# A gated two-layer block on one core: new order of ScalarE, VectorE and GpSimd work, and router logits in 16 products

## The chip, the cores and the metric

One NeuronCore of a Trainium2 chip runs the whole kernel. The metric is the time of the program on the device in microseconds. Three timed runs of the kernel before gave 561.67, 564.43 and 565.45 us; the median is 564.43.

## The reference

1024 tokens (4 x 256) of width 256 go through two layers, each an attention-like part and a feed-forward part, each part fed by a layer norm and added back through a tanh gate. Cut to what matters:

```python
x = x + tanh(g_xattn[0]) * _L0_xattn_ref(_layernorm(x), ids, ctx, ctx, ctx)   # 4 gated experts of 256, chosen by token id
x = x + tanh(g_ffn[0])   * _L0_ffn_ref(_layernorm(x), w_gate, w_up, w_down)   # BitNet: int8 tokens, ternary weights
x = x + tanh(g_xattn[1]) * _L1_xattn_ref(_layernorm(x), ctx, Wq, Wk, Wv, Wo)  # 8 x 128 tokens, 16 heads of 128
x = x + tanh(g_ffn[1])   * _L1_ffn_ref(_layernorm(x), gate_w, gate_bias, fc1_w, fc2_w, w1, w2, shared_up_w, shared_down_w)

# _L0_ffn_ref
gate = act_quant(x) @ weight_quant(w_gate).T         # act_quant: 128 / max|x| per token, rounded, clipped
up   = act_quant(x) @ weight_quant(w_up).T
y    = act_quant(fwht(silu(gate) * up)) @ weight_quant(w_down).T    # fwht: Walsh-Hadamard over 1024

# _L1_ffn_ref, 32 experts in 4 groups
scores = sigmoid(x @ gate_w.T)                       # the logits
sb     = scores + gate_bias
# per group: sum of the best two; the best two groups stay; of them the best 8 experts
cw     = scores of the chosen / their sum * 2.5      # 0 elsewhere
x_lat  = x @ fc1_w.T
h      = relu(x_lat @ w1[e].T)**2 * cw[:, e]         # for each of the 32 experts
out    = sum_e(h @ w2[e].T) @ fc2_w.T + relu(x @ shared_up_w.T)**2 @ shared_down_w.T
```

## The kernel before, in words

The tokens are NT = 8 tiles of 128, in NG = 2 halves of GN = 4 tiles (GT = 512 tokens). Each engine has a program of its own, written out in one function per engine, and they meet only at semaphores; an engine does its instructions in the order of the code. Matrices that must be exact to float32 are split into a high part (rounded to fp32r, mostly on ScalarE) and a low part (the rest, on VectorE or GpSimd), and one product is three TensorE passes: high by high, high by low, low by high (`product`, lines 1618 to 1624).

**Stages.** First the chosen experts of layer 0, then the BitNet feed-forward part, then 32 rounds u (16 heads by two halves of the batch) of attention, then 64 units i of the expert stage (32 experts for each half). The router and shared experts of the first half are done as tasks inside the last rounds of attention (`TASK_IN_STEP`), those of the second half inside the first units of the expert stage (`TASK_IN_UNIT`).

**Key/value units.** Beside the early stages TensorE computes keys and values of the attention, in units of 512 columns, numbered k. `FILLS` says how many units come behind which step of TensorE ("s0" to "d6"), and `FILL_AT[key]` which they are. TensorE's unit k waits for `kv_taken` >= k - 1, that is, until ScalarE (`take_unit`, the copy at L851) has copied the unit two before it out of the two PSUM banks they share. SyncE stores each copy (`store`), and the parts come back later as `k_hl` and `v_hl`, whose low parts are GpSimd's `key_low` (L598) and `value_low` (L604). Step "u0" waits for `y0_taken`, the last use of pair 0 in the stage before.

**Weight blocks.** All later weights come in 33 blocks of 512 KB in the order of `BLOCKS`: keys, values, queries, outputs, then the shared ones (S, D) and eight of the experts (E). For each, SyncE loads `blk_raw` (`load_block`, issued at L438, which waits until the block before is wholly taken), ScalarE makes the high part (`block_high`, L843) and GpSimd the low part (`block_low`, L592). Where each is done is written by hand in the feed-forward part, and by the tables `STEP_OF_BLOCK`, `UNIT_OF_BLOCK` (high), `LOW_UNIT_OF_BLOCK` (low) and `LOAD_AT_ROW` (the load, counted in rows `cw_row` of the router's weights that SyncE also loads, one per expert unit) later on. Blocks 29 to 32 hold the last sixteen experts.

**Feed-forward part.** Per tile there are TensorE stages: G (gate), U (up), H (the last Hadamard product), F (turn of the 1024 values into `fT`), C (the rounded values `q_b` turned back), D (down product); `STAGES` gives each its lag, and the list `FFN` the order, with the units "W" in between. ScalarE does silu (L954), `fT_hi` (L974) and `q` (L982); VectorE `inner` (`inner_values`, L1294), the maximum of the Hadamard result (L1434), `fT_lo`, `q_b` (L1457) and the update of `xr` (L1451); GpSimd the butterflies `fly` and `inner` (L650 to L656). The tokens of the first half are rounded by VectorE (`quantise(0)`); those of the second by ScalarE (`second_tokens`, L930), after VectorE's `token_scales(1)`, and TensorE turns them (L1836).

**PSUM pairs.** G, U, H, F and C each take a pair of banks from the list `free` in turn (`pair_of`), and before TensorE writes it waits for the one who used it last. While units stand behind "f1" no unit needs pair 0, so it is put into the list at ("W", "f1") and taken out at ("W", "d4"), where TensorE waits for its last user (`wait_freed(last_user[0])`).

**Router.** Task N normalises the tiles, L makes the logits (24 products of 32 columns per half: 4 tiles by 2 chunks by 3 passes), which ScalarE reads out of PSUM with its exponential (`logits_exp`); VectorE makes the scores (`scores_of_experts`), adds of the best two (`best_of_groups`), GpSimd the group mask (`mask_groups`, from L710), VectorE the best experts (`best_experts`), GpSimd the choice (`choose`), VectorE their sum (`wden`, L1392), GpSimd the weights `cw` (L744) and a root of them by Newton steps (L752 ends it), and task C turns them (L1998). They are stored (`store_weights`) and read back row by row. Tasks X and U are the latent tokens and the shared expert.

## Time and profile before

| | us |
|---|---|
| three timed runs | 561.67, 564.43, 565.45 |
| median | 564.43 |
| profiled execution, whole | 564.64 |
| its span (first to last instruction) | 562.8 |

All times in the rows below are of the profiled execution, counted from the start of its span. PE is TensorE (PEld its weight loads), DVE VectorE, ACT ScalarE, POOL GpSimd, and SPq the queue on which SyncE issues transfers. A wait is put down to the instruction whose end released it. PEclk is the granted clock of TensorE as a share of full speed, averaged over the window.

### The profile page before, as it was taken

The page shows a single profiled execution, that of the slowest core. Times are in us where ns is not written, and L with a number is a line of the kernel's source. Part 1 is how long each engine was busy: PE and PEld are TensorE (multiplying, and loading weights), DVE is VectorE, ACT ScalarE, POOL GpSimd, SP SyncE. Part 2 cuts the span into 40 slices and gives each one's busy share as a digit, 9 for nine tenths or more (in the row PEclk, how much of TensorE's full clock was granted, in tenths as well). Part 3 has the DMA queues.
Part 4 walks back from the last instruction along what each step waited for, and adds up shares of the span by engine and source line. Part 5 has one row for each costly group of instructions (what it writes and reads, how often), then busy time and mean ns, then how long its engine had stood idle before and what let it go on. Part 6 is the DMA issues. An engine that isn't in the chain of part 4 may idle for free.

```text
span 562.8 us, 9680 instructions
## 1 busy us (share of the span) xinstructions
PE 537.2 (95%) x3250; PEld 460.8 (82%) x3250; DVE 385.1 (68%) x815; ACT 355.4 (63%) x741; POOL 323.9 (58%) x325
## 2 busy tenths in 40 slices
PE   8999997998989999999999999999999989899997
PEld 6778765776778988998999999999999868677886
DVE  4858993699856576655655576636765857878883
ACT  4652245675678777766756565736766655787882
POOL 2679255899358697755645324425787465762320
PEclk9999998999999999999999999989999989999999
DMA  8911144610158677877577666524454745346751
GB/s 268 378 54 54 59 151 120 198 39 1 43 177 235 206 208 237 277 227 225 198 238 233 197 205 202 188 78 150 153 185 137 252 118 152 114 144 191 224 175 39
DMA packets 66544, 94.73 MB, mean 168 GB/s; under 512 B 6336, under 2 KB 38976, under 8 KB 66496
## 3 DMA queue, kind: packets, MB, share of 16 engines
q1 hardware_dynamic: 66496, 94.12, 52.6%
q8 instruction: 27, 0.44, 0.3%
q14 instruction: 21, 0.17, 0.1%
HBM read 66.71 MB, written 27.39 MB: 167 GB/s over the span
## 4 chain that ended last, share of the span: by engine, by line
PE 66%; DVE 17%; ACT 5%; issue 5%; POOL 4%; DMA 2%; SPq 0%; DVEq 0%; ACTq 0%; POOLq 0%
PE ps L1622 20%; PE ps L1623 19%; PE ps L1624 19%; PE ps L1754 4%; DVE xr L1230 2%; PE ps L1861 2%; DVE st L1135 1%; DMA xr<-in_x 1%; PE ps L1845 1%; DVE h L1165 1%; DMA cw_row<-cw_scratch 1%; DVE inner L1294 1%; DVE am L1434 1%; DVE e_lo L1547 1%; DVE e_r L1537 1%
## 5 line engine op out<-in xcount | busy, mean ns | idle before, releaser
L674 POOL TENSOR_TENSOR probs<-probs,rsum 128x512 f32<-128x512 f32 x64 | 66.6, 1044 | 57.6 <-DVE rsum L1318 57.5
L1313 DVE TENSOR_REDUCE nmax<-ps 128x2 f32<-128x512 f32 x64 | 44.0, 687 | 33.5 <-PE ps L1624 33.1
L1011 ACT ACTIVATE probs<-ps,nmax 128x256 f32<-128x256 f32 x128 | 59.9, 481 | 1.7 <-DVE nmax L1313 1.6
L1097 ACT ACTIVATE e_hi<-e_r 128x512 fp32r<-128x512 f32 x64 | 40.3, 629 | 31.0 <-DVE e_r L1537 30.0
L592 POOL TENSOR_TENSOR kv_w_lo<-blk_raw,kv_w_hi 128x1024 fp32r<-128x1024 f32 x16 | 38.8, 2424 | 36.2 <-ACT kv_w_hi L843 27.6
L1537 DVE SCALAR_TENSOR_TENSOR e_r<-ps,cw_row 128x512 f32<-128x512 f32 x64 | 43.6, 684 | 14.2 <-PE ps L1624 12.0
L1304 DVE TENSOR_TENSOR pT_lo<-ps,pT_hi 128x512 fp32r<-128x512 f32 x64 | 43.8, 685 | 12.8 <-ACT pT_hi L1017 12.2
L797 POOL TENSOR_TENSOR e_lo<-e_sq,e_hi 128x512 fp32r<-128x512 f32 x19 | 24.6, 1296 | 44.2 <-ACT e_sq L1103 39.3
L1309 DVE TENSOR_TENSOR oT_lo<-ps,oT_hi 128x512 fp32r<-128x512 f32 x32 | 22.1, 692 | 39.8 <-ACT oT_hi L1021 39.8
L1017 ACT ACTIVATE pT_hi<-ps 128x512 fp32r<-128x512 f32 x64 | 38.3, 601 | 15.8 <-PE ps L1754 15.6
L598 POOL TENSOR_TENSOR k_hl<-k_hl 128x512 fp32r<-128x512 f32 x20 | 26.0, 1298 | 37.1 <-ACT k_hl L938 37.0
L1021 ACT ACTIVATE oT_hi<-ps 128x512 fp32r<-128x512 f32 x32 | 19.1, 598 | 40.5 <-PE ps L1624 40.5
L1754 PE MATMUL ps<-eye,probs 128*128 128x128 f32 x256 | 39.0, 275 | 1.6 <-DVE kv_out L1344 1.0
L1622 PE MATMUL ps<-pT_hi,v_hl 128*128 128x256 f32 x128 | 36.7, 287 | 1.4 <-DVE hT_lo L1350 0.9
L853 ACT ACTIVATE kv_hi<-ps 128x512 fp32r<-128x512 f32 x36 | 21.7, 603 | 25.2 <-PE ps L1624 25.2
L1622 PE MATMUL ps<-k_hl,qT_lo 128*128 128x256 f32 x128 | 37.3, 291 | 0.0
L1624 PE MATMUL ps<-k_hl,qT_hi 128*128 128x256 f32 x128 | 36.3, 284 | 0.0
L1623 PE MATMUL ps<-wo_lo,oT_hi 128*128 128x256 f32 x128 | 36.2, 283 | 0.0
L1622 PE MATMUL ps<-wo_hi,oT_lo 128*128 128x256 f32 x128 | 36.2, 283 | 0.0
L1624 PE MATMUL ps<-pT_hi,v_hl 128*128 128x256 f32 x128 | 36.2, 283 | 0.0
L1623 PE MATMUL ps<-k_hl,qT_hi 128*128 128x256 f32 x128 | 36.2, 283 | 0.0
L1624 PE MATMUL ps<-wo_hi,oT_hi 128*128 128x256 f32 x128 | 36.2, 283 | 0.0
(311 smaller groups left out, 1873.6 us busy)
## 6 DMA issues: line engine op xcount, KB each, us to landing
cw_row<-cw_scratch SPq DMA_DIRECT2D x64, 256.0 KB, 3.4
v_hl<-v_scratch SPq DMA_DIRECT2D x24, 512.0 KB, 3.6
blk_raw<-in_w_blocks SPq DMA_DIRECT2D x22, 512.0 KB, 4.5
k_scratch<-kv_out SPq DMA_DIRECT2D x32, 256.0 KB, 2.6
v_scratch<-kv_out SPq DMA_DIRECT2D x32, 256.0 KB, 3.2
v_scratch<-kv_hi SPq DMA_DIRECT2D x24, 256.0 KB, 2.5
k_hl<-k_scratch SPq DMA_DIRECT2D x12, 512.0 KB, 3.5
k_hl<-k_scratch SPq DMA_DIRECT2D x20, 256.0 KB, 4.6
```

What stands on the lines that cost most here:

```text
L592: nc.gpsimd.tensor_tensor(lo[:, :], blk_raw[j % 2][:, :], hi[:, :].bitcast(F32), ALU.subtract).then_inc(blk_done, 1)
L674: nc.gpsimd.tensor_tensor(probs[:, b, :, :], probs[:, b, :, :], rsum[:, b, :].unsqueeze(2).to_broadcast([P, 2, S]), ALU.mult).then_inc(pro ...
L1011: last = nc.scalar.activation(probs[:, b, t, :], ps[:, S_BANK[b], t * S:(t + 1) * S], ACT.Exp, bias=nmax[:, b, t:t + 1], accum_out=esum[:, ...
L1017: nc.scalar.activation(pT_hi[:, b, :, :].rearrange("p k q -> p (k q)"), ps[:, P_BANK[b], :], ACT.Copy).then_inc(p_hi_done, 1)
L1097: nc.scalar.activation(e_hi[i % 4][:, :], e_r[i % 2][:, :], ACT.Square).then_inc(e_hi_done, 1)
L1304: V.tensor_tensor(pT_lo[:, b, :, :].rearrange("p k q -> p (k q)"), ps[:, P_BANK[b], :], pT_hi[:, b, :, :].rearrange("p k q -> p (k q)").bi ...
L1313: V.tensor_reduce(nmax[:, b, :], ps[:, S_BANK[b], :].rearrange("p (t k) -> p t k", t=2), AX.X, ALU.max, negate=True).then_inc(max_done, 1)
L1537: V.scalar_tensor_tensor(e_r[i % 2][:, :], ps[:, UP_BANK[i % 4], :], 0.0, cw_row[i % 4][:, :], ALU.max, ALU.mult).then_inc(root_done, 1)
L1622: mm(dst, l_lo, r_hi, start=first, stop=False, **kw)
L1623: mm(dst, l_hi, r_lo, start=False, stop=False, **kw)
L1624: return mm(dst, l_hi, r_hi, start=False, stop=last, **kw)
L1754: last = nc.tensor.transpose(ps[:, P_BANK[b], k * S + t * P:k * S + (t + 1) * P], probs[:, b, t, k * P:(k + 1) * P], ident)
```

## The change

The edits, by the names above:

1. **First tiles of the feed-forward part.** ScalarE no longer rounds the second tokens inside the units of "u1", but behind block 4, the first `fT_hi` and the first unit of "f0". VectorE's `token_scales(1)` is cut in two: the maximum (`token_maxima(1)`) first, then the first tile's low part (`turned_low(0)`), then the scales. `FILLS` moves the two units of "u0" to "g1" (three there), and with them the wait for `y0_taken`. Pair 0 enters `free` at place 2 instead of 0, so other stages use it.
2. **Scale of the Hadamard result.** The factor for `q` is min(128 / maximum, `c_most`) instead of being worked out from the clipped scale; `c_most` is new, one small operation per half.
3. **Blocks 5 to 7 and the key parts.** `BLOCKS` moves the first Q block from place 5 to 7. GpSimd does block 5 after tile 2, block 6 after tile 5 and nothing after tiles 3 and 6; `key_low(0)`, `key_low(1)` and `value_low(0)` come behind the last tile. ScalarE's `block_high(8)` moves from behind the queries to tile step 9, and the first turn of probabilities (`probs_back(0, 0)`) drops the wait for `kv_split`.
4. **Logits.** `gw_hi` and `gw_lo` lie side by side in `gw_hl`, 64 columns, so that a high token chunk meets both in one product: 16 products per half. VectorE adds the two column groups (`logits_add`, two operations, with a wait on the new `logit_added`), and ScalarE's exponential works in SBUF.
5. **Expert stage.** Tasks N, L, X and U stand at units 7, 9, 11, 12, 14, 16, 18 and 20 (before 6, 8, 10, 11, 13, 15, 17, 19), with the steps of VectorE, ScalarE and GpSimd for them one unit later; C stays at 23, as do `weight_sum` and the roots at 17. Blocks 29 to 32 are made at units 8, 9, 11, 13 (before 6, 7, 10, 16), and loads 31 and 32 issued at rows 15 and 17 (before 13, 16). `store_weights(1)` is issued before row 31, and its completion awaited before row 32.

The diff, cut:

```diff
-        BLOCKS = [("K", 0), ("V", 0), ("K", 1), ("V", 1), ("K", 2), ("Q", 0), ("K", 3), ("V", 2), ("O", 0), ("Q", 1), ("V", 3),
+        BLOCKS = [("K", 0), ("V", 0), ("K", 1), ("V", 1), ("K", 2), ("K", 3), ("V", 2), ("Q", 0), ("O", 0), ("Q", 1), ("V", 3),
...
-        UNIT_OF_BLOCK = {0: 28, 6: 29, 7: 30, 10: 31, 16: 32}
-        LOAD_AT_ROW = {4: 29, 8: 30, 13: 31, 16: 32}
+        UNIT_OF_BLOCK = {0: 28, 8: 29, 9: 30, 11: 31, 13: 32}
+        LOAD_AT_ROW = {4: 29, 8: 30, 15: 31, 17: 32}
...
-        FILLS = {"s0": 4, "s1": 2, "a11": 1, "y2": 1, "y6": 4, "u0": 2, "g1": 1, "u1": 3, "f0": 3, "g2": 1, "f1": 2, "d4": 1, "d5": 1, "c6": 1, "d6": 1}
+        FILLS = {"s0": 4, "s1": 2, "a11": 1, "y2": 1, "y6": 4, "g1": 3, "u1": 3, "f0": 3, "g2": 1, "f1": 2, "d4": 1, "d5": 1, "c6": 1, "d6": 1}
...
             if u == ("W", "f1"):
-                free.insert(0, 0)
+                free.insert(2, 0)
...
                 if n == 0:
                     block_low(4)
-                elif n in (2, 3):
-                    block_low(3 + n)
+                elif n == 2:
+                    block_low(5)
                 elif n == 5:
-                    key_low(0)
-                elif n == 6:
-                    value_low(0)
+                    block_low(6)

             pool.wait_ge(h_ready, NG + 1)
             block_low(7)
+            pool.wait_ge(q2_clipped, NT)
+            key_low(0)
             key_low(1)
+            value_low(0)
             block_low(8)
...
                     take("g" + str(i))
-                    if i == 1:
-                        second_tokens()
-                    else:
-                        take("u" + str(i))
+                    take("u" + str(i))
...
+                if i == NT + 1:
+                    block_high(8)
...
                 if i == 1:
-                    take("f0")
+                    take_unit(FILL_AT["f0"][0])
+                    second_tokens()
+                    for k in FILL_AT["f0"][1:]:
+                        take_unit(k)
...
                 if i == 1:
+                    last = token_maxima(1)
+                    turned_low(0)
+                    own(last)
                     token_scales(1).then_inc(q1_scaled, 1)
...
+                    own(V.reciprocal(a[:, 2:3], a[:, 0:1]))
+                    V.tensor_scalar(a[:, 2:3], a[:, 2:3], 128.0, c_most[:, n:n + 1], ALU.mult, ALU.min).then_inc(s2_ready, 1)
                     own(V.tensor_scalar(a[:, 1:2], a[:, 0:1], c_up[:, n:n + 1], Q_EPS, ALU.mult, ALU.max))
-                    own(V.reciprocal(a[:, 0:1], a[:, 1:2]))
-                    V.tensor_scalar(a[:, 2:3], a[:, 0:1], 128.0, c_up[:, n:n + 1], ALU.mult, ALU.mult).then_inc(s2_ready, 1)
...
-                    pe.wait_ge(kv_split, FILL_AT["e0"][-1] + 1 - FRONT_UNITS)
+                    if b:
+                        pe.wait_ge(kv_split, FILL_AT["e0"][-1] + 1 - FRONT_UNITS)
...
+            def logits_add(g, bank):
+                dve.wait_ge(logit_filled, g + 1)
+                parts = ps[:, bank, 0:2 * GN * E].rearrange("p (n two e) -> p n two e", n=GN, two=2)
+                own(V.tensor_copy(sc[:, :, :], parts[:, :, 0, :]))
+                V.tensor_tensor(sc[:, :, :], parts[:, :, 1, :], sc[:, :, :], ALU.add).then_inc(logit_added, 1)
...
+                        mm(ps[:, bank, wide], hT_hi[:, 0, tokens], gw_hl[:, 0, :], start=True, stop=False)
                         for c in range(DC):
-                            last = product(ps[:, bank, j * E:(j + 1) * E], both(hT_hi, hT_lo, A, c, slice(t * P, (t + 1) * P)),
-                                           both(gw_hi, gw_lo, A, c, A), c == 0, c == DC - 1)
+                            mm(ps[:, bank, narrow], hT_lo[:, c, tokens], gw_hl[:, c, 0:E], start=False, stop=False)
+                        last = mm(ps[:, bank, wide], hT_hi[:, 1, tokens], gw_hl[:, 1, :], start=False, stop=True)
```

**ScalarE, first two tiles.** Its rows from the second silu (`inner`) on, before; `kv_out` is the copy of a key/value unit, `qtok` the second tokens' rounding, `kv_w_hi` block 4.

```order
L954 ACTIVATE inner<-ps,c_gate 128x1024
L851 ACTIVATE kv_out<-ps 128x512 x2
L930 ACTIVATE qtok<-h,am_r 128x256 x4
L851 ACTIVATE kv_out<-ps 128x512 x2
L843 ACTIVATE kv_w_hi<-blk_raw 128x1024
L974 ACTIVATE fT_hi<-ps 128x1024
L851 ACTIVATE kv_out<-ps 128x512 x3
```

And now, from the first two silus on:

```order
L953 ACTIVATE inner<-ps,c_gate 128x1024 x2
L853 ACTIVATE kv_out<-ps 128x512 x6
L845 ACTIVATE kv_w_hi<-blk_raw 128x1024
L972 ACTIVATE fT_hi<-ps 128x1024
L853 ACTIVATE kv_out<-ps 128x512
L931 ACTIVATE qtok<-h,am_r 128x256 x4
L853 ACTIVATE kv_out<-ps 128x512 x2
```

The rounding moved from between the copies of "u1" to behind `fT_hi` and one copy of "f0"; the copies that stood between the two silus follow the second.

**GpSimd, end of the feed-forward loop.** Its rows behind the butterflies (`fly`, `inner`) of the sixth tile, before; `k_hl` and `v_hl` are key and value parts, `kv_w_lo` and `wq_lo` low parts of blocks.

```order
L598 TENSOR_TENSOR k_hl<-k_hl 128x512
L650 TENSOR_TENSOR fly<-inner 128x512
L651 TENSOR_TENSOR fly<-inner 128x512
L655 TENSOR_TENSOR inner<-fly 128x2x256
L656 TENSOR_TENSOR inner<-fly 128x2x256
L604 TENSOR_TENSOR v_hl<-v_hl 128x512
L650 TENSOR_TENSOR fly<-inner 128x512
L651 TENSOR_TENSOR fly<-inner 128x512
L655 TENSOR_TENSOR inner<-fly 128x2x256
L656 TENSOR_TENSOR inner<-fly 128x2x256
L592 TENSOR_TENSOR kv_w_lo<-blk_raw,kv_w_hi 128x1024
L598 TENSOR_TENSOR k_hl<-k_hl 128x512
```

And now, from the same place on:

```order
L593 TENSOR_TENSOR kv_w_lo<-blk_raw,kv_w_hi 128x1024
L651 TENSOR_TENSOR fly<-inner 128x512
L652 TENSOR_TENSOR fly<-inner 128x512
L656 TENSOR_TENSOR inner<-fly 128x2x256
L657 TENSOR_TENSOR inner<-fly 128x2x256
L651 TENSOR_TENSOR fly<-inner 128x512
L652 TENSOR_TENSOR fly<-inner 128x512
L656 TENSOR_TENSOR inner<-fly 128x2x256
L657 TENSOR_TENSOR inner<-fly 128x2x256
L593 TENSOR_TENSOR wq_lo<-blk_raw,wq_hi 128x1024
L599 TENSOR_TENSOR k_hl<-k_hl 128x512 x2
L605 TENSOR_TENSOR v_hl<-v_hl 128x512
```

A block's low part took the place of the key part behind the sixth tile, nothing stands behind the seventh, and both key parts and the value part come behind the last tile.

**GpSimd, expert stage of the second half.** Its rows at units 4 to 12, before; `e_lo` is its share of the expert values, `ex_lo` are blocks 31 and 32, `sbias` the biased scores, `gscore` the first step of `mask_groups`.

```order
L797 TENSOR_TENSOR e_lo<-e_sq,e_hi 128x512 x2
L592 TENSOR_TENSOR kv_w_lo<-blk_raw,kv_w_hi 128x1024
L592 TENSOR_TENSOR wo_lo<-blk_raw,wo_hi 128x1024
L797 TENSOR_TENSOR e_lo<-e_sq,e_hi 128x512 x2
L592 TENSOR_TENSOR ex_lo<-blk_raw,ex_hi 128x1024
L704 TENSOR_TENSOR sbias<-sc,gbias 128x128
L710 TENSOR_TENSOR gscore<-gtop 128x16
```

And now:

```order
L799 TENSOR_TENSOR e_lo<-e_sq,e_hi 128x512 x3
L593 TENSOR_TENSOR kv_w_lo<-blk_raw,kv_w_hi 128x1024
L593 TENSOR_TENSOR wo_lo<-blk_raw,wo_hi 128x1024
L799 TENSOR_TENSOR e_lo<-e_sq,e_hi 128x512
L593 TENSOR_TENSOR ex_lo<-blk_raw,ex_hi 128x1024
L706 TENSOR_TENSOR sbias<-sc,gbias 128x128
L593 TENSOR_TENSOR ex_lo<-blk_raw,ex_hi 128x1024
L712 TENSOR_TENSOR gscore<-gtop 128x16
```

Block 32's low part, which stood behind the masks and the best experts, now stands in front of `mask_groups`.

## Rows read from the trace of the kernel before

**Rows 1.** The page: busy time of each engine, its share of the span, instructions

```profile
PE 537.2 (95%) x3250; PEld 460.8 (82%) x3250; DVE 385.1 (68%) x815; ACT 355.4 (63%) x741; POOL 323.9 (58%) x325
```

**Rows 2.** TensorE's waits, by releaser: us in total, times, longest

```profile
PE ps L1622 <- ACT kv_out L851: 3.1, 1, 3.1
PE ps L1974 <- DVE h L1337: 2.4, 1, 2.4
PE ps L1622 <- DVE xr L1451: 2.0, 1, 2.0
...
PE ps L1622 <- DVE s_sq L1363: 1.4, 1, 1.4
...
PE ps L1754 <- DVE kv_out L1344: 1.0, 1, 1.0
...
PE ps L1836 <- issue: 0.7, 1, 0.7
PE ps L1622 <- DVE xr L1230: 0.7, 1, 0.7
```

**Rows 3.** Windows: length, busy PE, PEld, DVE, ACT, POOL, PEclk, DMA share, GB/s

```profile
90.00:100.00 10.00, 10.00 (x44) 7.37 (x44) 2.42 (x4) 5.37 (x8) 7.37 (x5) 0.83 0.61 158
360.00:380.00 20.00, 19.79 (x140) 18.43 (x139) 10.19 (x19) 10.82 (x30) 6.72 (x6) 0.91 0.40 132
440.00:460.00 20.00, 17.55 (x87) 14.20 (x86) 14.48 (x31) 12.32 (x21) 11.70 (x20) 0.91 0.58 177
460.00:480.00 20.00, 20.00 (x108) 16.90 (x108) 13.71 (x36) 12.46 (x22) 12.58 (x19) 1.00 0.52 156
```

**Rows 4.** Timeline, 78 to 90 us: start, duration, instruction, [idle before, releaser]

```profile
78.01 1.20 DVE L1146 TENSOR_SCALAR ln_i<-ln_v 128x4 int32<-128x4 int32 x1
...
85.78 1.21 DVE L1269 TENSOR_REDUCE am<-h 128x4 f32<-128x1024 f32 x1
...
87.45 1.70 ACT L930 ACTIVATE qtok<-h,am_r 128x256 f32<-128x256 f32 x4 [3.72 <-DVE am_r L1271]
```

**Rows 5.** Feed-forward loop: timeline, and `q_b` in ns min/median/max

```profile
117.97 1.11 ACT L982 ACTIVATE q<-ps,am 128x1024 f32<-128x1024 f32 x1
119.14 1.04 PE L1845 MATMUL ps<-wq,qT 128*128 128x512 bf16 x4 [0.46 <-ACT q L982]
135.05 1.27 POOL L604 TENSOR_TENSOR v_hl<-v_hl 128x512 fp32r<-128x512 f32 x1
...
L1457 DVE TENSOR_SCALAR q_b<-q x8: 682/1302/1764, 103.8 to 153.3; 128x1024 bf16<-128x1024 f32 x8
```

**Rows 6.** Timeline at the start of attention

```profile
160.75 2.40 POOL L592 TENSOR_TENSOR wo_lo<-blk_raw,wo_hi 128x1024 fp32r<-128x1024 f32 x1 [6.79 <-ACT wo_hi L843]
161.64 1.28 ACT L1011 ACT_TABLE_LOAD   x1
...
167.12 0.63 ACT L938 ACTIVATE k_hl<-k_hl 128x512 fp32r<-128x512 f32 x1 [0.78 <-DMA k_hl<-k_scratch]
```

**Rows 7.** TensorE's timeline, last output product, first and last of 24 logits products

```profile
367.75 0.28 PE L1624 MATMUL ps<-wo_hi,oT_hi 128*128 128x256 f32 x1
367.87 0.18 PE L1622 MATMUL ps<-gw_hi,hT_lo 128*128 128x32 f32 x1
...
370.36 0.26 PE L1624 MATMUL ps<-gw_hi,hT_hi 128*128 128x32 f32 x1
```

**Rows 8.** Expert stage: timeline; then loads (L438) from 400 us on, landing

```profile
461.06 0.33 SPq L438 DMA_DIRECT2D blk_raw<-in_w_tail  x1
475.43 0.22 POOL L710 TENSOR_TENSOR gscore<-gtop 128x16 f32<-128x16 f32 x1 [2.37 <-DVE gtop L1375]
484.68 2.30 DVE L1392 SCALAR_TENSOR_TENSOR wden<-wden 128x4 f32<-128x4 f32 x1
496.27 0.30 PE L1998 MATMUL ps<-eye,cw 128*128 128x128 f32 x1 [0.74 <-POOL cw L752]
...
DMA to landing us min/median/max: 3.2/5.6/6.6
```

More of the change, by code:

```diff
@@ L136, in flamingo_two_layer_kernel @@
         c_up = sb("c_up", [P, NT], F32, region)
+        c_most = sb("c_most", [P, NT], F32, region)
         qtok = sb("qtok", [P, GN, D], F32, region)
@@ L507, in _ @@
             load_block(4)
-            store("u0")
             load_block(5)
@@ L931, in second_tokens @@
                 last.then_inc(q1_rounded, 1)
-                for k in FILL_AT["u1"][1:]:
-                    take_unit(k)
             def key_high(u):
@@ L1025, in norm_chunk_high, with logits_exp @@
                 nc.scalar.activation(hT_hi[:, c, g * GT:(g + 1) * GT], ps[:, bank, :], ACT.Copy).then_inc(hT_hi_done, 1)
[L1027 to L1030 removed]
+            def logits_exp(g):
+                act.wait_ge(logit_added, g + 1)
+                nc.scalar.activation(sc[:, :, :], sc[:, :, :], ACT.Exp, scale=-1.0).then_inc(logit_exp, 1)
             def latent_high(g, bank):
@@ L1264, in _, with token_maxima @@
                 V.tensor_tensor(z_lo[:, g, :, :], a_sel[:, g, :, :], z_hi[:, g, :, :].bitcast(F32), ALU.subtract).then_inc(z_done, 1)
+            def token_maxima(g):
+                s = slice(g * GN, (g + 1) * GN)
+                return V.tensor_reduce(am[:, s], h[:, s, :], AX.X, ALU.max, apply_absolute_value=True)
             def token_scales(g):
                 s = slice(g * GN, (g + 1) * GN)
-                own(V.tensor_reduce(am[:, s], h[:, s, :], AX.X, ALU.max, apply_absolute_value=True))
                 own(V.tensor_scalar(am_c[:, s], am[:, s], Q_EPS, 1.0 / 128.0, ALU.max, ALU.mult))
@@ L1278, in quantise @@
                 else:
+                    own(token_maxima(0))
                     own(token_scales(0))
@@ L1285, in quantise @@
                 V.tensor_scalar(q1[:, :, :], qtok[:, :, :], ROUND, 127.0, ALU.subtract, ALU.min).then_inc(q1_ready, 1)
-                V.tensor_scalar(c_up[:, s], am_c[:, s], wmean[:, 1:2], None, ALU.mult)
+                own(V.tensor_scalar(c_up[:, s], am_c[:, s], wmean[:, 1:2], None, ALU.mult))
+                V.tensor_scalar(c_most[:, s], c_up[:, s], 128.0, 1.0 / Q_EPS, ALU.mult, ALU.mult)
                 V.tensor_scalar(c_gate[:, s], am_c[:, s], wmean[:, 0:1], None, ALU.mult).then_inc(scales_ready, 1)
@@ L1295, in inner_values, with turned_low @@
                                 ALU.mult).then_inc(inner_done, 1)
+            def turned_low(n):
+                b = pair_of["F", n]
+                dve.wait_ge(fT_hi_done, n + 1)
+                V.tensor_tensor(fT_lo[:, :, :].rearrange("p c t -> p (c t)"), ps[:, b:b + 2, :].rearrange("p a n -> p (a n)"),
+                                fT_hi[:, :, :].rearrange("p c t -> p (c t)").bitcast(F32), ALU.subtract).then_inc(fT_done, 1)
             def query_low(u):
@@ L1688, in fill_units @@
                         pe.wait_ge(a_taken, (NB - 1) * NG)
-                    if key == "u0":
+                    if key == "g1":
                         pe.wait_ge(y0_taken, NT)
```

76 lines of the change are left out of this document (37 added, 39 removed).

## The prediction

> **What bounds the kernel now.** I read the page's busy table first: TensorE is busy for 537 of 562.8 us [rows 1], so time falls only where TensorE gets less work, waits less, or runs at full clock. Next come TensorE's waits [rows 2]: the longest are 3.1 us for a ScalarE copy of a key/value unit, 2.4 us for the normalised tiles of the second half in the expert stage, 2.0 us for an update of `xr` at the end of the feed-forward part, 1.4 us for a `s_sq` and 1.0 us for a `kv_out`. Then the windows with the granted clock [rows 3]: it falls from 2.4 to 1.2 GHz behind the 3.1 us wait, and once more between 360 and 380 us, where TensorE hardly waited but had run the small router products. The loss is (1 - PEclk) times the window: 0.17 x 10 = 1.7 us between 90 and 100, 0.09 x 20 = 1.8 us between 360 and 380, and 1.8 us again between 440 and 460, behind the 2.4 us wait.
>
> The sum is made against the profiled execution, 564.6 us (span 562.8 and 1.8 around it); the median of the runs, 564.4, lies 0.2 below it, so I take the difference from 564.6. About 1%, 5.6 us, is what a measurement of this kernel can tell from no change.
>
> **1. First tiles (70 to 107 us).** Before, ScalarE's rounding of the second half's tokens stood in front of two unit copies: VectorE's maximum at 85.78 us, 1.2 us long, then scaling, then rounding from 87.45 for 1.7 us [rows 4]; the copies came after it, and TensorE, which may be two units ahead only, stood 3.1 us. Now ScalarE does all six copies, the block and the tile's high part first. Walking the new order with the old durations: unit copies to 85.4 us, block 4 to 86.4, `fT_hi` to 87.4, the first `f0` unit to 88.0; VectorE's low part to 88.7 and scales to 89.2; rounding (1.7) to 90.9; second `f0` unit to 91.5. TensorE reaches the `g2` unit, which needs that copy, at 90.6. So 0.9 of the 3.1 stays: 2.2 us won, and the clock's 1.7 with it, since no wait near its 3 us is left there (behind the 2.0 us wait the clock stayed). Units 12 to 14 move behind the second gate product, so the 0.7 us wait for VectorE's `xr` is filled with it, and the turn of the second tokens (`L1836`, 0.7 of issue) is no longer in pair 0, whose copy it waited for: 0.7 each. Sum 2.2 + 1.7 + 0.7 + 0.7 = **5.3 us**. Bounds: 3.0, if the wait only moves and the clock falls still; 7.0, if nothing is left of any wait.
>
> The scale reordering (reciprocal first, `c_most`) publishes the factor one small operation of 0.2 us earlier. In the loop it buys nothing: `q` starts at 117.97 behind ScalarE's own `fT_hi`, and TensorE's second product waits for that `q` until 119.14 [rows 5]. It counts once, at the last tile: 0.2 us. The added `c_most` is one such small operation per half, beside other waits; bounds 0 and 0.4.
>
> **2. End of the feed-forward loop (125 to 156 us).** The 2.0 us wait goes: pair 0 now ends with the last "up" result, which VectorE frees as it multiplies tile 7, and not with the `xr` update of tile 4, which is later in its queue. What is late next is GpSimd: block 6's low part (2.4 us) stands behind the sixth tile instead of a value part (1.3, [rows 5]), so the seventh tile's turn comes 1.1 us later, and with it the q of tile 5. Following it through: the last Hadamard product starts 0.7 us earlier than before. With the 0.2 above, **0.9 us**; bounds -1 and 2.5. The first key's two parts and the value's one (1.3 us each) and the Q block (2.4) come behind the tiles, where GpSimd was idle for 6.8 us [rows 6]; it walks to about 155 us for the first key, before the first scores. VectorE's `q_b` took 0.68 to 1.76 us for one shape [rows 5]; the last, 1.23 us, ran beside a key part that is now behind it. The Trainium skill, "SBUF — State Buffer", section "Who interferes with whom", says that a VectorE operation in a two-port mode and a GpSimd operation exclude each other for a whole instruction; the spread above agrees. It takes the last `q_b` to 0.7 us, which is hidden by ScalarE's `c6` copy and `hT_hi`, so the sum is the same by it.
>
> **3. Start of attention (159 to 168 us).** Block 8's high part (1.05 us) leaves the queue in front of the exponent table's load at 161.64 [rows 6] for an idle stretch of ScalarE near 150, and the first probabilities' turn drops its wait of 1.0 us for `kv_out`. Walked with the old durations, the probabilities are ready at 165.5 then, and TensorE comes to them at 166.4. But ScalarE next waits for a key load (0.78 us idle before 167.12), which comes no earlier; the slack behind it is about 1 us. **1.0 us**; bounds 0 and 2.
>
> **4. Logits.** 24 products of 32 columns start 0.108 us apart, (370.36 - 367.87) / 23 [rows 7], and one of 256 columns in front of them takes 0.12, so 64 columns cost nearly the same. Eight go: 0.87 us in each half. The Trainium skill, "TensorE: Matmul & The Clock Gate", section "Back-to-back issue gap", gives N / 2.4 GHz + 2.5 ns, an estimate of 16 ns for 32 columns; by it the eight would be worth 0.1 us. Its figure is not what the row shows here, and the row decides. The clock's fall behind them costs 1.8 us in the first half; the same 24 in the second half, between 460 and 480, ran at 1.00 throughout [rows 3]. I count it half gone: 0.9. First half **1.7 us**; bounds 0 and 2.7. The logits' sum on VectorE (two small operations) lies beside 1.4 us of expert products.
>
> **5. Expert stage of the second half (450 to 506 us).** On TensorE much goes: of the 2.4 us wait for the normalised tiles 0.9 stays, as one more expert unit (six products of 512 columns, by the 0.12 us of 256 columns in [rows 7] about 1.4 us) runs in front of the turn; the half clock behind it (1.8); 0.9 of logits; 1.4 for `s_sq`. But the router's result, the transposed weights at 496.27, sets the end, and GpSimd's `cw` released it after a wait of 0.74 [rows 8]. That chain runs logits, `sc`, masks (475.43 on), best experts, `wden` (484.68), roots. Walking it: block 29's low part ends near 464.5, not 461.0, so block 31's load is issued there. It lands in 3.2 us at best, as at 461.06, and 5.6 is the median of the seven from 400 us on. ScalarE, which reaches block 31 at 467.2, waits there, with logits' exponential and the latent high part queued behind it and VectorE waiting for them; scores at 471 to 472.4, the groups' best at 475.5, as before (475.4). Then GpSimd has block 32's low part (2.4 us) in front of the masks: they start at 478.3, 2.9 us late. What is given back: `wden` took 2.30 us beside a block's low part and now 0.3. Masks to 482.4, best to 483.6, choice to 485.4, `wden` to 486.9, exactly where it ended before. Roots are unchanged, 9 us. So the transposed weights stay at about 496.3: TensorE's gains turn into a wait there. What is left is the store of the weights before row 31 and its wait after it: **0.4 us**. Bounds: -3.5 (load of 6.6 us) and 5.5 (the chain not late at all).
>
> Sum: 5.3 + 0.9 + 1.0 + 1.7 + 0.4 = 9.3 us; 564.6 - 9.3 = **555.3 us**.
>
> **Rivals.**
> A (forecast): as above, 555.3, own range 552.5 to 558. Chance 0.50.
> B: the router's chain is not the bound, since blocks 31 and 32 get in between its steps; the expert stage then gives 1.5 (wait), 1.8 (clock), 0.9 (logits), 1.4 (`s_sq`), less the 0.4 counted: 5.2 more, 550.1. For it: `wden`'s 2.3 us collision goes. Against it: block 32 stands in GpSimd's queue before the masks. Chance 0.20.
> C: the first tiles give only their half. If GpSimd's block 4 holds up the two scaling operations on VectorE (such a small one took 1.20 us at 78.01 beside GpSimd [rows 4]), the rounding is 1.1 later, TensorE waits 2 us and the clock falls again (1.7); the late seventh tile eats the 0.9. 555.3 + 1.1 + 1.7 + 0.9 = 559.0. Chance 0.25.
> D, slower than before: one mechanism, ScalarE stopped at blocks 31 and 32 by their loads. It decides if both land in 6.6 us, the longest seen, instead of 3.2: 3.4 twice on the router's chain, and two falls of the clock at 1.7 behind TensorE's waits: 10.2 us, which is more than the 9.3 won; 565.5. Against it: few rows are in flight there. Chance 0.05.
> That the change does not do what it says: the 64-column products could cost more than the 32-column ones; between 0.108 and the 0.12 of 256 columns that is at most 0.1 us, so it has no case of its own.
>
> **Numbers.** Range 549.5 to 560.5: B's value at one end, C's with its spread at the other; D and the outer half of B are left out. Faster by over 1% (under 559.0): nearly all of A, all of B, half of C, 0.79. Within 1%: the rest of A and C, most of D, 0.18. Slower by over 1%: D with more on top, 0.03.
>
> **What would show it.** Step 1: no wait over 1 us and PEclk 1.00 between 85 and 100, the turn of the second tokens (`L1836`, second time) 5 to 6 us earlier than before. Step 2: no wait for `xr` L1451's successor, but `F` of tile 6 waiting for GpSimd. Step 3: the first turn of probabilities straight behind the scores. Step 4: 16 products in 1.8 us. Step 5: ScalarE idle before `ex_hi`, GpSimd's masks behind `ex_lo`, and a wait of 1 to 3 us before the transpose of `cw`. The forecast is wrong if the first wait is still over 2 us with a half clock behind it, or if the transpose of `cw` runs without a wait and over 4 us earlier relative to the start of the stage.

## The result, and the profile after

The changed kernel takes 555.05 us (median of four runs, 554.75 to 556.06) where before took 564.51 in the same session (four runs, 561.67 to 565.45): the medians lie 9.5 us apart. The ratio of the runs is 0.9842 (95% interval 0.9818 to 0.9865), which is 8.9 us. Its profiled execution took 554.95 us with a span of 553.2, 9.6 less than the span before.

TensorE's busy time fell by 4.4 us from [rows 1], to the line below. The other 5.2 of the 9.6 us were idle time:

```profile
PE 532.8 (96%) x3234; PEld 456.5 (83%) x3234; DVE 385.1 (70%) x821; ACT 354.3 (64%) x741; POOL 323.8 (59%) x325
```

TensorE's waits of the changed kernel (us in total, times, longest):

```profile
PE ps L1645 <- DVE xl_lo L1368: 2.0, 1, 2.0
PE ps L2024 <- POOL cw L754: 1.7, 1, 1.7
```

Of [rows 2] the 3.1 us for a unit copy, the 2.0 for `xr`, the 1.0 for `kv_out` and both 0.7 are gone, and the 2.4 for the normalised tiles has shrunk to 0.4; the 1.4 for `s_sq` is as before. New are 2.0 us for `xl_lo`, the low part of the latent tokens, and the wait for `cw` has grown from 0.7 [rows 8] to 1.7; both are in the expert stage. Windows that answer to [rows 3], with the same columns (PEclk is the third number from the end):

```profile
90.00:100.00 10.00, 9.98 (x60) 7.42 (x59) 8.32 (x12) 6.40 (x11) 8.49 (x8) 1.00 0.68 189
...
360.00:380.00 20.00, 20.00 (x141) 18.56 (x140) 12.11 (x24) 11.76 (x32) 8.24 (x8) 1.00 0.41 134
...
460.00:480.00 20.00, 16.55 (x65) 12.72 (x64) 16.44 (x51) 10.77 (x21) 13.26 (x26) 0.91 0.31 107
```

The clock stays at 2.4 GHz in the first tiles and behind the first half's logits (PEclk 1.00), and PEclk is 1.00 between 440 and 460 us too. In the expert stage it still falls once to 1.2 GHz for a time, only later, behind the 2.0 us wait (PEclk 0.50 between 464 and 466).

How much each stretch gave is read by taking the same instruction in both traces and subtracting its start. A "turn" is a transposition by TensorE:

| instruction on TensorE | before | after | gained so far | this stretch | forecast |
|---|---|---|---|---|---|
| first turn of second tokens | 105.06 | 99.66 | 5.40 | 5.4 | 5.3 |
| first product of the queries, behind the last `hT` | 156.02 | 149.46 | 6.56 | 1.2 | 0.9 |
| first turn of probabilities | 167.38 | 159.68 | 7.70 | 1.1 | 1.0 |
| first logits product | 367.87 | 360.22 | 7.65 | 0.0 | |
| last turn of probabilities | 431.92 | 421.83 | 10.09 | 2.4 | 1.7 |
| turn of `cw`, second half | 496.27 | 486.40 | 9.87 | -0.2 | |
| end of the span | 562.8 | 553.2 | 9.6 | -0.2 | 0.4 |

Two executions of unchanged code agree closely by this measure. Over the kernels below that share the changed kernel's first 99 us, that first turn lies between 99.46 and 99.67 in all but two (100.28 and 100.01, where everything from the first tiles on is shifted). From there to the first turn of probabilities they all take 60.0 or 60.1 us, and on to the first logits product 200.3 to 200.5 (experiments 8 and 12, whose edits lie in the first of these stretches, left out). So a difference in these stretches is good to 0.1 or 0.2 us, better than the whole times. It is not so later on. From the last turn of probabilities to the turn of `cw`, kernels with the same code there take 64.3 to 65.1 us, and from the turn of `cw` to the end 66.8 to 68.7 (the changed kernel and experiments 1 to 3, 8 and 12).

### The profile page after: what moved, and what is told of

The parts are those of the page before. It is cut to its first block, busy times and chain, and to the rows that moved or that the text cites. A ratio compares the mean times of both kernels' runs of the same rounds, so it can differ in the third digit from the quotient of the medians.

```text
span 553.2 us, 9654 instructions
## 1 busy us (share of the span) xinstructions
PE 532.8 (96%) x3234; PEld 456.5 (83%) x3234; DVE 385.1 (70%) x821; ACT 354.3 (64%) x741; POOL 323.8 (59%) x325
## 4 chain that ended last, share of the span: by engine, by line
PE 65%; DVE 14%; POOL 8%; issue 5%; ACT 5%; DMA 2%; SPq 0%; DVEq 0%; POOLq 0%; ACTq 0%
PE ps L1645 20%; PE ps L1646 19%; PE ps L1647 19%; PE ps L1778 4%; DVE xr L1231 2%; DMA xr<-in_x 1%; DVE st L1136 1%; POOL kv_w_lo L593 1%; DMA blk_raw<-in_w_tail 1%; POOL inner L657 1%; POOL inner L656 1%; DVE h L1166 1%; ACT kv_w_hi L845 1%; POOL s_lo L681 1%; POOL fly L651 1%
```

## The experiments

Unless it says otherwise, each is the changed kernel with one edit. "Before" beside it gave 564.59, 563.91 and 564.0 us in the three sessions.

**1. The rounding back in its old place.**

```diff
-                    take("u" + str(i))
+                    if i == 1:
+                        take_unit(FILL_AT["u1"][0])
+                        second_tokens()
...
-                    take_unit(FILL_AT["f0"][0])
-                    second_tokens()
...
-                    last = token_maxima(1)
-                    turned_low(0)
-                    own(last)
+                    own(token_maxima(1))
```

> The changed kernel (555.05 us) with one part undone: ScalarE rounds the second tokens inside the units of u1 again, and VectorE makes their maximum and scales before the first tile's low part. Theory (the forecast's step 1): the wait for a unit copy comes back at about 3 us with the half clock behind it: 3.9 us more, 559.0 us (558 to 560), PEclk about 0.83 between 85 and 100 us, and the turn of the second tokens about 4 us later than 99.66. Rival: it was the new place of the two units and of pair 0 that took the wait away, and the rounding's place matters little: less than 1.5 us more, PEclk 1.00 there.

Measured: 561.92 us (561.25 to 562.83), 6.9 more than the changed kernel, and the turn of the second tokens at 105.45, 5.8 later. TensorE's longest wait and the windows of this kernel:

```profile
PE ps L1646 <- ACT kv_out L853: 4.0, 1, 4.0
```

```profile
80.00:90.00 10.00, 6.04 (x32) 4.68 (x29) 7.81 (x19) 3.66 (x8) 1.89 (x2) 0.94 0.22 82
90.00:100.00 10.00, 10.00 (x33) 7.14 (x34) 1.64 (x4) 5.56 (x8) 7.38 (x5) 0.72 0.50 143
```

The theory's mechanism holds (the wait and the half clock both return), its size does not. The wait is 4.0 us and not 3.1, since the units at "g1" bring TensorE to it 0.8 us earlier (at 85.91 us instead of 86.70) while VectorE's maximum comes when it did (85.87 us against 85.78). The 0.06 x 10 in the first window cost nothing: TensorE stood until 89.87, and the clock had fallen only in the last microsecond or so before that. From 89.87 to 100 PEclk is 0.71, so the half clock costs 0.29 x 10.1 = 2.9 us, against the 1.7 of [rows 3]. Wait and clock are 6.9 us; less the 0.5 us wait for block 4's low part, which the changed kernel has here and this one has not, 6.4. Of these, 5.8 show at the turn, and the other 0.6 were not traced. Of the span's 6.9 us, 1.3 come behind the turn of `cw` (68.1 us to the end instead of 66.8; see experiment 8).

**2. Pair 0 back at the head of the list.**

```diff
-                free.insert(2, 0)
+                free.insert(0, 0)
```

> The changed kernel with pair 0 put back to the head of the free list. Theory (steps 1 and 2): the turn of the second tokens waits 0.7 us for its pair again, and the unit at d4 waits for the update of xr again (2.0 us before): 0.7 plus what step 2 won by it, 0.9 to 2.0: 556.7 to 557.8 us. Rival: GpSimd's late seventh tile would hide the wait at d4: only 0.7 us more, 555.8 us. Second rival: the place in the list does not matter, within 0.3 us.

Measured: 557.84 us (556.85 to 558.92), 2.8 more. The turn of the second tokens starts at 100.50 (0.8 later), the first turn of probabilities at 161.86 (2.2 later). TensorE's waits of this kernel have both rows of [rows 2] back:

```profile
PE ps L1645 <- DVE xr L1472: 2.0, 1, 2.0
...
PE ps L1860 <- issue: 0.7, 1, 0.7
```

The theory holds: one number in a list takes away two waits that are 35 us apart.

**3. Two units back at u0.**

```diff
-        FILLS = {..., "y6": 4, "g1": 3, "u1": 3, ...
+        FILLS = {..., "y6": 4, "u0": 2, "g1": 1, "u1": 3, ...
...
+            store("u0")
...
-                    if key == "g1":
+                    if key == "u0":
                         pe.wait_ge(y0_taken, NT)
```

> The changed kernel with two units back at u0 (u0: 2, g1: 1) and the wait for y0_taken with them. Theory (step 1): the 0.7 us wait for VectorE's xr comes back in front of u0: 0.7 us more, 555.8 us; the turn of the second tokens at 100.4 us of the span. Rival: the wait only moves (the later units stand at their copies anyway): 0.0, turn at 99.7. Against both: if the order also sets the rounding's cover, 2 us or more with a wait for kv_out.

Measured: 556.97 us (555.68 to 558.79), 1.9 more by the medians, 1.2 by the spans; the turn of the second tokens at 100.60, 0.94 later, with the 0.7 us wait for `xr` back. The theory holds at the turn (0.7 was expected there); the medians' 1.9 us are more than it, with runs that spread over 3 us.

**4. 24 logits products.**

```diff
-                        mm(ps[:, bank, wide], hT_hi[:, 0, tokens], gw_hl[:, 0, :], start=True, stop=False)
                         for c in range(DC):
-                            mm(ps[:, bank, narrow], hT_lo[:, c, tokens], gw_hl[:, c, 0:E], start=False, stop=False)
-                        last = mm(ps[:, bank, wide], hT_hi[:, 1, tokens], gw_hl[:, 1, :], start=False, stop=True)
+                            mm(ps[:, bank, narrow], hT_lo[:, c, tokens], gw_hl[:, c, 0:E], start=c == 0, stop=False)
+                            mm(ps[:, bank, narrow], hT_hi[:, c, tokens], gw_hl[:, c, E:2 * E], start=False, stop=False)
+                            last = mm(ps[:, bank, narrow], hT_hi[:, c, tokens], gw_hl[:, c, 0:E], start=False, stop=c == 1)
...
-                V.tensor_tensor(sc[:, :, :], parts[:, :, 1, :], sc[:, :, :], ALU.add).then_inc(logit_added, 1)
+                V.tensor_scalar(sc[:, :, :], sc[:, :, :], 0.0, None, ALU.add).then_inc(logit_added, 1)
```

> The changed kernel with 24 products of 32 columns for the logits of each half in place of 16, all into the first column group; the sum on VectorE stays as two operations of the same size (the second adds 0). Theory (step 4, with the clock's fall wholly in it): 0.9 us for eight products and 1.8 for the clock in the first half, nothing in the second, where the wait for the weights cw absorbs it: 2.7 us more, 557.7 us, PEclk 0.91 in the window of 20 us around the first half's logits. Rival A: the number of products costs only themselves: 0.9 us more, 555.9 us, PEclk 1.00. Rival B: both halves lose both: 5 us more, 560 us.

Measured: 558.43 us (558.06 to 558.76), 3.4 more. First to last logits product takes 2.49 us (1.59 with 16), and from the first of them to the last turn of probabilities 64.08 us against 61.61: 2.5 us, 0.9 of products and 1.6 of clock. The rest of the span's 3.2 lies behind the turn of `cw` (67.7 us to the end instead of 66.8), where the kernels scatter. The windows, first of this kernel, the last of them behind the second half's logits (455.87 to 458.43):

```profile
360.00:366.00 6.00, 6.00 (x40) 5.62 (x39) 2.50 (x5) 1.51 (x6) 0.00 (x0) 0.78 0.25 91
...
460.00:462.00 2.00, 2.00 (x6) 1.58 (x5) 0.87 (x2) 1.20 (x2) 0.54 (x1) 0.50 0.92 253
```

then of the changed kernel:

```profile
360.00:366.00 6.00, 6.00 (x48) 5.70 (x47) 3.00 (x6) 2.60 (x9) 0.21 (x1) 1.00 0.27 91
```

Its 16 products start 0.106 us apart on the mean (360.22 to 361.81, fifteen steps), the 24 of this kernel 0.108, so 64 columns cost what 32 do. TensorE stands still in neither window, and the granted clock is 0.78 behind 24 products and 1.00 behind 16. The theory with the whole fall (2.7 us) holds for the first half, not the forecast's half. In the second half it is wrong on one point: the clock falls there too (PEclk 0.50 between 460 and 462, about 1.7 us between 458 and 464), though behind the same 24 products of the kernel before it stayed at 1.00 [rows 3]. That costs nothing in the time, as the theory has it: the turn of `cw` comes 2.3 us later, no more than the first half's 2.5.

**5. The expert stage as before.** Tables, tasks and steps of edit 5 undone (the store of the weights ahead of row 31 kept), logits at 16 products.

```diff
-        UNIT_OF_BLOCK = {0: 28, 8: 29, 9: 30, 11: 31, 13: 32}
+        UNIT_OF_BLOCK = {0: 28, 6: 29, 7: 30, 10: 31, 16: 32}
...
-        LOAD_AT_ROW = {4: 29, 8: 30, 15: 31, 17: 32}
+        LOAD_AT_ROW = {4: 29, 8: 30, 13: 31, 16: 32}
...
-        TASK_IN_UNIT = {7: ("N", 0), 9: ("N", 1), 11: ("L", 0), 12: ("X", 0), 14: ("U", 0), ...
+        TASK_IN_UNIT = {6: ("N", 0), 8: ("N", 1), 10: ("L", 0), 11: ("X", 0), 13: ("U", 0), ...
...
```

> The changed kernel with the expert stage's tables and steps of before (tasks at units 6, 8, 10, 11, 13, ..., blocks 29 to 32 at units 6, 7, 10, 16, loads at rows 13 and 16); the logits stay at 16 products. From the start of attention's last rounds on, the changed kernel's stage took 0.2 us more than before up to the turned weights. Theory (the router's chain sets the end, with block 32's low part in front of the masks weighed up by the wden of 2.3 us beside a low part): the old order ends within 1 us of the new, 554 to 556 us, with the 2.4 us wait for the normalised tiles back and no long wait for cw. Rival: TensorE's gains of the new order reach the end: 3 us or more slower, 558 us. Rival 2: block 32 in front of the masks is a plain loss: 2.5 us faster, 552.5 us.

Measured: 552.67 us (552.1 to 552.91), 2.4 less than the changed kernel. So edit 5, all but its store, is a loss of 2.4 us: the second rival's number is right, its reason only in part (experiment 6). GpSimd's timeline in the changed kernel, with the load and ScalarE's block 31 beside it:

```profile
453.85 0.33 SPq L438 DMA_DIRECT2D blk_raw<-in_w_tail  x1
...
458.07 1.06 ACT L845 ACTIVATE ex_hi<-blk_raw 128x1024 fp32r<-128x1024 f32 x1 [1.69 <-DMA blk_raw<-in_w_tail]
...
466.02 2.40 POOL L593 TENSOR_TENSOR ex_lo<-blk_raw,ex_hi 128x1024 fp32r<-128x1024 f32 x1 [2.81 <-ACT ex_hi L845]
468.38 0.21 POOL L712 TENSOR_TENSOR gscore<-gtop 128x16 f32<-128x16 f32 x1
```

and with the old stage:

```profile
462.94 0.22 POOL L712 TENSOR_TENSOR gscore<-gtop 128x16 f32<-128x16 f32 x1 [2.38 <-DVE gtop L1395]
...
472.19 2.30 DVE L1412 SCALAR_TENSOR_TENSOR wden<-wden 128x4 f32<-128x4 f32 x1
```

The masks begin 13.0 us after the last logits product (455.36) in the changed kernel and 8.8 us after it (454.10) with the old stage. The old stage gives 1.6 of that lead back at `wden`, 2.30 us against 0.70, beside block 32's low part. `cw` is turned at 483.75 instead of 486.40, 2.6 us earlier. In both, TensorE waits for `cw` (0.75 and 1.67 us), so GpSimd's chain sets that turn, and TensorE's other waits and its clock show in the time only where they hold this chain up. The two lie close, though: in experiments 1, 2 and 12, whose stage is the changed kernel's, TensorE waits 2.9 or 3.0 us for `s_sq` instead of 1.4 and comes to the turn of `cw` when it is done.

**6. Block 32 at unit 20.**

```diff
-        UNIT_OF_BLOCK = {0: 28, 8: 29, 9: 30, 11: 31, 13: 32}
+        UNIT_OF_BLOCK = {0: 28, 8: 29, 9: 30, 11: 31, 20: 32}
```

(and the same in `LOW_UNIT_OF_BLOCK`)

> The changed kernel with block 32 (high and low part) at unit 20 instead of 13, nothing else. Theory: GpSimd starts the masks 2.4 us earlier, as the low part stood straight in front of them (466.02 to 468.38 us of the span), ScalarE has 1.0 us more room, the 1.7 us wait for cw goes: 1.7 us faster (1.2 to 2.4), 553.3 us. Rival: another step of the chain is late instead (the best experts on VectorE, or the roots' own length with shared parts between them), and the time stays at 555.

Measured: 555.06 us (553.26 to 556.21), no change. The masks start at 465.87, 2.5 us earlier, and the turn of `cw` at 483.87, 2.5 earlier, as the theory says; but the way from the turn of `cw` to the end is 69.0 us instead of 66.8, and all but 0.3 of the 2.5 is gone at the end. In it TensorE waits for block 32 itself:

```profile
487.37 0.50 PE L1645 MATMUL ps<-xl_hi,ex_lo 128*128 128x512 f32 x1 [1.13 <-POOL ex_lo L593]
```

So a new wait took part of the gain, a different one from those the rival named. The other half of the loss was not traced; SyncE's stores of the weights took 2.83 us to issue instead of 1.72, but that pair of numbers does not go with the end in other kernels (last section).

**7. Block 32 at unit 20 and block 31 at unit 12.**

```diff
-        UNIT_OF_BLOCK = {0: 28, 8: 29, 9: 30, 11: 31, 13: 32}
+        UNIT_OF_BLOCK = {0: 28, 8: 29, 9: 30, 12: 31, 20: 32}
```

(and the same in `LOW_UNIT_OF_BLOCK`)

> As the kernel with block 32 at unit 20, and block 31 at unit 12 instead of 11, so that ScalarE's logits exponential and latent high part no longer queue behind the wait of 1.7 us for block 31's load. Theory: the whole chain starts 1.7 to 2.7 us earlier, TensorE's 2.0 us wait for xl_lo goes and the half clock behind it (0.9 of 10 us at most 1.8): 3 to 5 us faster than the changed kernel, 550 to 552 us. Rival: only the wait for xl_lo goes and another wait takes its place (s_sq, cw): within 1 us of the kernel with block 32 alone.

Measured: 551.05 us (550.12 to 551.69), ratio to before 0.9774 (0.9743 to 0.9805), 4.0 less than the changed kernel: the best of all, and the theory holds. GpSimd's timeline:

```profile
460.86 2.40 POOL L593 TENSOR_TENSOR ex_lo<-blk_raw,ex_hi 128x1024 fp32r<-128x1024 f32 x1
463.27 0.22 POOL L712 TENSOR_TENSOR gscore<-gtop 128x16 f32<-128x16 f32 x1
```

Now it is block 31's low part that fills GpSimd's time until the groups' best. The masks begin 8.0 us after the last logits product, as before the change, and `cw` is turned at 481.26, 5.1 us earlier than in the changed kernel. Of these, 1.8 are gone at the end (68.6 us instead of 66.8, with the 1.1 us wait for block 32 again). The wait for `xl_lo` is gone, and PEclk is 1.00 between 460 and 480.

**8. The start of attention as before.**

```diff
-                if i == NT + 1:
-                    block_high(8)
...
+            block_high(8)
             block_high(9)
...
-                    if b:
-                        pe.wait_ge(kv_split, FILL_AT["e0"][-1] + 1 - FRONT_UNITS)
+                    pe.wait_ge(kv_split, FILL_AT["e0"][-1] + 1 - FRONT_UNITS)
```

> The changed kernel with ScalarE's high part of block 8 behind the queries again and the wait for kv_split back in front of the first turn of probabilities. Theory (step 3): 1.0 us more (0.5 to 1.5), 556.0 us, with a wait of about 1 us in front of the first turn. Rival: the gain came from the key parts behind the tiles or from VectorE's q_b, and these two cost nothing: within 0.3 us.

Measured: 557.26 us (556.29 to 557.75), 2.2 more. The first turn of probabilities, again with its wait:

```profile
160.68 0.52 PE L1776 MATMUL ps<-eye,probs 128*128 128x128 f32 x3 [0.93 <-DVE kv_out L1357]
```

It starts 1.00 later than in the changed kernel, as the theory has it, and 0.6 of it is left at the turn of `cw`. The other 1.9 us of the span's 2.5 arise behind that turn, where the kernels scatter by as much; so the 2.2 us of the medians, above the theory's 0.5 to 1.5, are not shown to be the edit's. There VectorE waits for row 32 of the weights, first in the changed kernel, then here:

```profile
494.86 0.69 DVE L1558 SCALAR_TENSOR_TENSOR e_r<-ps,cw_row 128x512 f32<-128x512 f32 x1 [1.35 <-DMA cw_row<-cw_scratch]
```

```profile
496.73 0.69 DVE L1557 SCALAR_TENSOR_TENSOR e_r<-ps,cw_row 128x512 f32<-128x512 f32 x1 [2.61 <-DMA cw_row<-cw_scratch]
```

**9. Loads of blocks 31 and 32 earlier.**

```diff
-        UNIT_OF_BLOCK = {0: 28, 8: 29, 9: 30, 11: 31, 13: 32}
+        UNIT_OF_BLOCK = {0: 28, 6: 29, 7: 30, 11: 31, 13: 32}
...
-        LOAD_AT_ROW = {4: 29, 8: 30, 15: 31, 17: 32}
+        LOAD_AT_ROW = {4: 29, 8: 30, 13: 31, 16: 32}
```

> The changed kernel with blocks 29 and 30 at units 6 and 7 again and the loads of 31 and 32 at rows 13 and 16; blocks 31 and 32 stay at units 11 and 13, tasks at their new units. Theory (what the changed kernel loses in the expert stage is ScalarE's wait of 1.7 us for block 31's load, with the logits' exponential behind it, and the masks behind block 32's low part): the loads are issued 3 us earlier, ScalarE no longer waits, scores 1.2 to 2 us earlier, block 32's low part falls into GpSimd's idle time before the groups' best, the transposed weights come at about 482.5 us of the span, 4 us earlier: 551.5 us (550.5 to 553). Rival: blocks 29 and 30 in units 6 and 7 delay the normalised tiles on ScalarE by as much (2 us): 554 to 555 us.

Measured: 555.02 us (554.28 to 555.45), no change; the rival is right. ScalarE no longer stands at block 31, but blocks 29 and 30 delay the turned tiles (TensorE's 1.5 us wait for `hT_lo`), the logits end 1.4 us later (456.76), and block 32's low part still comes straight before the masks, which start at 468.03:

```profile
465.67 2.42 POOL L593 TENSOR_TENSOR ex_lo<-blk_raw,ex_hi 128x1024 fp32r<-128x1024 f32 x1 [2.82 <-ACT ex_hi L845]
```

**10. The old expert stage with block 32 at unit 12.**

```diff
-        UNIT_OF_BLOCK = {0: 28, 6: 29, 7: 30, 10: 31, 16: 32}
+        UNIT_OF_BLOCK = {0: 28, 6: 29, 7: 30, 10: 31, 12: 32}
```

(against experiment 5, and the same in `LOW_UNIT_OF_BLOCK`)

> The expert stage of before (as in the run with its tables back, 552.67 us), with block 32 at unit 12 instead of 16. Theory: its low part of 2.4 us fits into the 2.4 us in which GpSimd waits for the groups' best (460.6 to 462.9 us of the span), and the 2.3 us of wden beside a low part go: the transposed weights at 481.6 us, 2.1 us earlier: 550.6 us (550 to 551.5). Rival: block 32's load (issued at 453.3) or ScalarE's 1 us for it is late, so that the low part runs into the masks: 552 to 553 us.

Measured: 552.41 us (551.76 to 554.2, five runs), no better than experiment 5; the rival is right. GpSimd idles 2.82 us for ScalarE's `ex_hi`, which stands behind expert values that wait for VectorE, and then does the low part ahead of the masks, which start at 466.42 (462.94 in experiment 5; this trace runs some 0.6 us late from the first tiles on):

```profile
464.05 2.42 POOL L593 TENSOR_TENSOR ex_lo<-blk_raw,ex_hi 128x1024 fp32r<-128x1024 f32 x1 [2.82 <-ACT ex_hi L845]
```

**11. As 10, and ScalarE copies the turned weights earlier.**

```diff
                if i in TASK_IN_UNIT and TASK_IN_UNIT[i][0] != "C":
                    take_task(1, TASK_IN_UNIT[i], 1)
+                if i == 22:
+                    take_task(1, ("C", 0), 1)
```

> As the kernel with the old expert stage and block 32 at unit 12, and ScalarE copies the turned weights in unit 22 ahead of its shared parts and squares instead of unit 23. Theory: the end of the stage hangs on copy, store, and the load of row 32 (VectorE waited 1.35 us for that row in the changed kernel, 2.61 in another run, and the time from the turned weights to the end went from 66.8 to 68.7 us with it): with the copy 2 us earlier the wait is gone and the tail is 66.5 us whatever the transfers do: 0.3 to 1.5 us faster than without it. Rival: TensorE's tail has its own waits (a low part of block 31 or 32, expert values) and does not shorten; or the delayed squares cost more: same or 0.5 slower.

Measured: 552.91 us (552.14 to 553.91, six runs), 0.5 more than experiment 10, with ranges that overlap: not told apart in the times. In the profiles the copy starts 1.35 us after the turn instead of 2.38, VectorE's wait for row 32 (1.40 in experiment 10) is gone, and the way from the turn to the end is 65.7 us instead of 66.9, the shortest of all. So the wait goes as the theory says; that it is worth anything in the time was not shown.

**12. Block 6 behind tile 3.**

```diff
-                elif n == 2:
-                    block_low(5)
-                elif n == 5:
-                    block_low(6)
+                elif n in (2, 3):
+                    block_low(3 + n)
```

> The changed kernel with GpSimd's low part of block 6 behind tile 3 instead of tile 5. Theory (step 2): a low part makes GpSimd's turn of 5.6 us longer than the loop's 6.4 us, 1.1 to 1.6 us late, and behind the fourth tile it is caught up by the seventh, so the waits for GpSimd in front of the turn of tile 6 (0.5) and the last Hadamard product (0.9) go: the last q_b turn 0.7 us earlier (146.9 us), 554.3 us. Rival: VectorE's and ScalarE's chain for the last tiles takes as long whatever GpSimd does: last turn at 147.6, 555 us.

Measured: 555.49 us (554.92 to 555.76), the last `q_b` turn at 147.87 instead of 147.62. The rival is right: TensorE's wait for GpSimd shrinks (0.5 to 0.2), but its waits before the Hadamard products, which the profile puts down to no engine, grow from 0.7 to 1.2, and the time does not shrink.

## Why the forecast was right, and where it was not

555.3 us was forecast and 555.05 measured. Steps 1 to 3 follow the trace one by one. That the sum came out so close is in part luck: step 4 gave 0.7 us more than forecast and step 5 0.8 less, and the two cancel.

**Step 1** (5.3; measured 5.4) is right in sum and sequence: the rounding starts at 89.46 us where 89.2 was walked. Of the 3.1 us wait 0.9 was to stay for a unit's copy; none stands there, and the only wait of TensorE above 0.3 us in this stretch is the 0.48 for GpSimd's block 4. Experiment 1 shows that without the rounding's move nothing of it is left (105.45 against 105.06 before), and experiments 1 to 3 that its parts don't add: undone singly they cost 5.8, 0.8 and 0.9 at the same instruction, 7.5 for a gain of 5.4. My reading is that the 0.7s of the units and the pair are worth nothing while TensorE stands at the rounding anyway; neither was tried alone on the kernel before. Rival C's collision with GpSimd took place only in part (`am_c` took 0.40 us) and stayed hidden.

**Step 2** (0.9; measured 1.2): that the pair's place removes the 2.0 us wait is shown by experiment 2. The reason given for the deduction, GpSimd's late seventh tile, falls with experiment 12, where GpSimd is less late and the last turn is not earlier. What holds back the last tiles then is not settled; 1.2 us of TensorE's wait for a low part of `hT` stand before the first query product. Which part the keys behind the tiles have in it was not tried, nor was edit 2 undone alone, to which the forecast gave 0.2 us.

**Step 3** (1.0; measured 1.1) is right, by experiment 8, where the first turn of probabilities comes 1.00 us later.

**Step 4** (1.7; measured 2.4): the mis-sized term is "I count it half gone". The products gave 0.9 as forecast, and the clock's fall went whole, 1.6 us, by experiment 4. The halving rested on the second half's 24 products, which had run at 1.00 in the kernel before; in experiment 4 the clock fell behind these too, so one trace in which it stays says little. The 16 ns a product that the forecast takes from the Trainium skill, "TensorE: Matmul & The Clock Gate", section "Back-to-back issue gap", is given there for a product standing alone; the section itself says that it counts too little for few columns when every product has its weight load, as here. The 0.106 us of experiment 4 agrees with that.

**Step 5** (0.4 gained; measured 0.4 lost): the chain was walked rightly. Put on the clock of before (10.1 us more), the load of block 31 is issued at 463.9 (forecast 464.5), the masks start at 478.5 (478.3), `cw` is turned at 496.5 (496.3), with a wait of 1.7 us in front (1 to 3). What the step did not see is that this end was a price and not a bound: "the transposed weights stay at about 496.3" was read as the router's chain holding the end wherever the edits stand. Experiments 5 and 7 end 2.4 and 4.0 us earlier with the same logits. So much of rival B's gain was there to be had (5.6 us in this stage; experiment 7 has 3.6, its 4.0 less the 0.4 lost, or 2.9 by the spans), and edit 5 gave it away: by 1.7 us of ScalarE waiting for a load with the logits' exponential behind it, and by 2.4 us of low part ahead of the masks. The shares of the two are not separated: with block 32 moved alone (experiment 6) the 2.5 us won at the turn were lost again behind it, with earlier loads (experiment 9) at the tiles, and block 31 moved alone was not tried, nor the store ahead of row 31 apart.

## What to carry to other kernels

Work out for each queue what stands behind an instruction that waits; a block of work that "fits" is free only if its input is there when the gap opens, and it is ahead of nothing that others wait for. When several edits remove waits at one place, undo each alone before crediting them with a sum: here the single prices added to 7.5 us for a gain of 5.4. Subtracting the start of one and the same instruction in two traces, stage by stage, finds 0.1 or 0.2 us where the whole times scatter by 1. Test first, on kernels with the same code there, in which stages it does: in the last one here it was good only to 2 us.

## What the runs showed of the hardware that was not expected

The length of a wait does not tell what the clock costs behind it. Behind 3.1 us of TensorE standing the half clock cost 1.7 us [rows 3], behind 4.0 us 2.9 (experiment 1). Behind 2.0 us it cost nothing at the end of the feed-forward part of the kernel before (PEclk 1.00 from 136 to 144 us) and about 1.7 us in the expert stage of the changed kernel (0.90 over the 16.7 us from the end of the wait to 480). And the clock falls behind 24 small products in three cases out of four, in experiment 4's first half without any wait near it, and not behind 16: in the changed kernel and the eleven experiments that have 16, PEclk is 1.00 from 360 to 380 us and from 452 to 462. Whether it is the number of products or the wider ones that keep it up was not tried apart.

A tiny VectorE operation can last as long as GpSimd's instruction beside it. `c_most`, 4 numbers per partition, in the changed kernel (GpSimd busy from 93.34 to 94.61), then in experiment 1 (GpSimd idle until 91.23):

```profile
93.44 1.20 DVE L1293 TENSOR_SCALAR c_most<-c_up 128x4 f32<-128x4 f32 x1
```

```profile
90.14 0.17 DVE L1296 TENSOR_SCALAR c_most<-c_up 128x4 f32<-128x4 f32 x1
```

The end of this kernel also hangs on transfers. From the turn of `cw` to the end it took 66.8 us in the changed kernel and 68.7 in experiment 8, with the same instructions in between; SyncE's four stores of the weights took 1.72 us to issue in the one and 2.67 in the other. That alone does not explain it: with 1.71 us for the stores the way was 68.1 us in experiment 1, and with 2.55 it was 67.0 in experiment 5. Why is open.
